# Three of nine experts of each pair of sequences run inside the next pair's layers, with the pair loop written out

## The chip, the cores and the metric

The kernel runs on one core of one Trainium2 chip. A core has five engines with an instruction stream each: TensorE (PE: matmuls and transposes; its weight loads are listed apart as PEld), VectorE (DVE), ScalarE (ACT), GpSimd (POOL) and SyncE (SP, which here only issues DMAs). They wait for one another through semaphores. The metric is the device time of one execution, in microseconds (us); lower is better.

## The reference, cut to what matters

Eight sequences of 256 tokens with 128 features pass through four layers. The change touches only the last stretch, in which two sequences (a pair, 512 tokens) are worked on together; what comes ahead is a linear-attention layer over single sequences.

```python
x = x + _L0_attn_ref(_layernorm(x), ...)      # before the pairs
x = x + _L0_ffn_ref(_layernorm(x), ...)       # 8 experts of 176 hidden + a shared one, top 2
x = x + _L1_attn_ref(_layernorm(x), ...)      # 16 heads of 8, causal, then a 128-512-128 MLP
x = x + _L1_ffn_ref(_layernorm(x), ...)       # the layer of the change:

def _L1_ffn_ref(x, shared_up, shared_down, routed_up, routed_down, router_w):
    H, F, E_SHARED, E_ROUTED, K = (128, 512, 1, 8, 2)
    def _expert(x, w_up, w_down):
        h = jax.nn.gelu(jnp.einsum('bsh,hf->bsf', x, w_up), approximate=False)
        return jnp.einsum('bsf,fh->bsh', h, w_down)
    ...                                        # gates: softmax, the two largest kept
    for e in range(E_ROUTED):
        routed_out = routed_out + gates[..., e:e + 1] * _expert(x, routed_up[e], routed_down[e])
    return shared_out + routed_out + x
```

The kernel computes all nine experts (one shared, eight routed) for all tokens, and weights each result by its gate, which is zero for an expert that was not chosen.

## The kernel before

The first half of the program (up to about 815 us) handles the eight sequences one after the other. Then come four pairs, `pair_layers(it, more)` on each engine. Pairs 0 to 2 are three rounds of a hardware loop (`Fori`), pair 3 stands behind the loop as code of its own. Order within an engine is the order of the code; there is no scheduler. One pair is, in TensorE's order:

- Start: `route(hT0, ...)` (8 columns of router scores, L1314), then 14 steps of the first feed-forward layer's up projections (L1330; each step two matmuls of 512 columns), its down projections (L1348, L1349, and L1358 to L1360) in four token chunks. VectorE adds the weighted results into `x2` chunk by chunk (L1894, L1900) and counts `merged`, once a chunk. Chunks 0 and 1 use banks 4, 5, 0, 1 of `ps` for expert results, chunks 2 and 3 banks 2 to 5; banks 6 and 7 hold the shared part.
- **Gap 1**: VectorE ends the last chunks and does two layer norms (`norm`, L1559 to L1572, with the inverse root on GpSimd, L508). `turn_tokens(1, h_tok, 4)` transposes the result (L1308), ScalarE copies it to `hT` (L830), and the attention begins with `a_wqkv` (L1365), the rotation on VectorE (L1923 to L1927) and the transposes L1374.
- Attention: scores (L1394, L1400) with maxima on VectorE (L1935), turned scores (L1428, L1432), exponentials on ScalarE (L881), values (L1452), output projection `a_wo` (L1489).
- **Gap 2**: VectorE takes the projection and does norm 5; `turn_tokens(2, h_tok, 5)`; then the MLP's up matmuls (L1494), four Gelus (L895), its down matmuls (L1499).
- **Gap 3**: VectorE adds that (L1956) and does norm 6; `turn_tokens(3, h_tok, 6)`, `route(hT, m_rt)` (L1314), and the experts.
- Experts 0 to 8: `up(e)` is four matmuls of 512 columns (L1513, in the trace 8 records, since each fp32 matmul is recorded twice), ScalarE's four Gelus (L903), `down(e)` 16 matmuls of 128 columns (L1522, 32 records), and VectorE adds bank 4 or 5, times the gate, into `x2` (L1977). `up(e + 1)` stands ahead of `down(e)`. After `down(4)` stands `turn_first(it + 1)` (L1300), the next pair's first transpose.

ScalarE holds one function table at a time; `load_table` (L832) switches it early. The names that the change and the prediction use are `h_tok` (normalised tokens), `hT` (their transpose, the input of every up matmul), `hid1` (two buffers for Gelu results), `x2` (the residual sum), `rw` (gates), `mgelu`, `mup_psum`, `mdown_psum`, `mdown_used` (counts of Gelus, up matmuls, down groups and additions).

Of the kernel before, what the change touches and what calls it, by code (L numbers as in the profile page):

```python
# [61 lines left out]
N_UP = HT1 * (E + 2)  # L62
N_DOWN = E + 2
# [15 lines left out]
DVE_STEPS2 = 161  # L79
POOL_STEPS2 = 1  # L80
# [40 lines left out]
def program(nc, t, out):  # L121
# [10 lines left out]
    with ExitStack() as ctx:  # L132
# [49 lines left out]
        def carve(phase, shape, at=None):  # L182
# [78 lines left out]
        rw = sb("rw", [P, G, E + 1])  # L261
        rwT = sb("rwT", [P, G * P])
# [22 lines left out]
        hT = carve(2, [G * P])  # L285
        v_aug = carve(2, [G, AH, AV])
# [29 lines left out]
            "mup_psum mgelu mdown_psum mlp_added mdown_used x_final x_stored "  # L316
# [51 lines left out]
        def _(sp):  # L368
# [38 lines left out]
            with sp.Fori(0, PAIRS - 1) as it:  # L407

                sp.wait_ge(s["merged"], G * it + G)
                sp.dma_start(pair_in[:, :, :], pair(out, it + 1)).then_inc(s["pair_loaded"], 16)  # L410
                sp.wait_ge(s["x_final"], it + 2)
                sp.dma_start(pair(out, it), x2[:, :, :]).then_inc(s["x_stored"], 16)
            sp.wait_ge(s["x_final"], PAIRS + 1)
            sp.dma_start(pair(out, PAIRS - 1), x2[:, :, :]).then_inc(s["x_stored"], 16)
            sp.wait_ge(s["x_stored"], 16 * PAIRS + 1)
# [3 lines left out]
        def _(pool):  # L419
# [17 lines left out]
            pool.memset(pool_pad[:, 1:2], 0.0).then_inc(s["x_stored"], 1)  # L437
            pool.memset(pool_pad[:, 2:3], 0.0).then_inc(s["x_final"], 1)
# [71 lines left out]

            def pair_layers(it, more):
                me = Steps(pool, s["pool_step2"], it, POOL_STEPS2)
# [12 lines left out]
                if more:  # L525
                    inverse_root(it + 1, 0)
                    assert me.n == POOL_STEPS2, ("POOL_STEPS2", me.n)

# [6 lines left out]
            with pool.Fori(0, PAIRS - 1) as it:  # L535
                pair_layers(it, True)
            pair_layers(PAIRS - 1, False)


        @block.scalar  # L540
        def _(act):
# [274 lines left out]

            def turned_first(i):

                act.wait_ge(s["hT_psum"], i * N_HT + 1)
                act.activation(hT0, ps[:, 7, :], ACT.Copy).then_inc(s["hT_ready"], 1)  # L820

            def pair_layers(it, more):
                def transpose_out(k, gb=None):
# [3 lines left out]
                    if gb is None:  # L827
                        act.activation(hT, src, ACT.Copy).then_inc(s["hT_ready"], 1)
# [4 lines left out]
                def load_table(function):  # L833

                    act.wait_ge(s["act_step"], it * 2 + (1 if function == ACT.Exp else 2))
                    act.activation(act_pad[:, :], act_pad[:, :], function).then_inc(s["act_step"], 1)

# [16 lines left out]

                load_table(ACT.Exp)
# [35 lines left out]
                load_table(ACT.Gelu)  # L891
                transpose_out(2, gb=1)
                for i in range(HT1):
                    act.wait_ge(s["mup_psum"], it * N_UP + i + 1)
                    act.activation(hid1[0][:, i, :], ps[:, i, :], ACT.Gelu, bias=a_b1[:, i:i + 1])\  # L895
                        .then_inc(s["mgelu"], 1)
# [3 lines left out]
                for e in range(E + 1):  # L900
                    for i in range(HT1):
                        act.wait_ge(s["mup_psum"], it * N_UP + HT1 * (e + 1) + i + 1)
                        act.activation(hid1[e % 2][:, i, :], ps[:, i, :], ACT.Gelu).then_inc(s["mgelu"], 1)  # L903
# [5 lines left out]
            with act.Fori(0, PAIRS - 1) as it:  # L909
                pair_layers(it, True)  # L910
            pair_layers(PAIRS - 1, False)


        @block.tensor
        def _(pe):
# [387 lines left out]
            def pair_layers(it, more):  # L1303
# [18 lines left out]
                for k, i in enumerate(UP_ORDER):  # L1322
# [3 lines left out]
                    if k == 2:  # L1326

                        pe.wait_ge(s["x_final"], it + 1)
# [32 lines left out]

                turn_tokens(1, h_tok, 4)
# [5 lines left out]
                def turn_qk(c):  # L1368
                    pe.wait_ge(s["rot_ready"], it * G + c + 1)
                    if c >= 2:  # L1370
                        pe.wait_ge(s["qT_ready"], (it * G + c - 1) * 2)
                    for q in range(2):
# [118 lines left out]
                mm.then_inc(s["wo_psum"], 1)  # L1491
                turn_tokens(2, h_tok, 5)
                for i in range(HT1):
                    pe.matmul(ps[:, i, :], a_w1[:, i * P:(i + 1) * P], hT, start=True, stop=True)\  # L1494
                        .then_inc(s["mup_psum"], 1)
                pe.wait_ge(s["mgelu"], it * N_UP + HT1)
# [4 lines left out]
                mm.then_inc(s["mdown_psum"], 1)  # L1501

                turn_tokens(3, h_tok, 6)
# [4 lines left out]
                def up(e):  # L1508
                    for i in range(HT1):
                        if e >= 1:  # L1510

                            pe.wait_ge(s["mgelu"], it * N_UP + HT1 * e + i + 1)
                        pe.matmul(ps[:, i, :], m_up[:, e, i * P:(i + 1) * P], hT, start=True, stop=True)\  # L1513
                            .then_inc(s["mup_psum"], 1)

                def down(e):
                    pe.wait_ge(s["mgelu"], it * N_UP + HT1 * (e + 2))
                    if e >= 2:
                        pe.wait_ge(s["mdown_used"], it * E + e - 1)
                    for c in range(G):  # L1520
                        for i in range(HT1):
                            mm = pe.matmul(ps[:, 4 + e % 2, c * P:(c + 1) * P], hid1[e % 2][:, i, c * P:(c + 1) * P],  # L1522
# [550 lines left out]
```

## Time and profile before

| | |
|---|---|
| Median of 3 timed runs | 1685.59 us (1682.43 to 1690.14) |
| Profiled execution: its own time | 1669.67 us |
| Its span in the trace | 1667.9 us |
| TensorE matmul busy | 1368.3 us (82%), 11040 instructions |
| TensorE weight load busy | 984.9 us (59%) |
| VectorE busy | 911.9 us (55%) |
| ScalarE busy | 723.2 us (43%) |
| GpSimd busy | 195.3 us (12%) |
| Granted TensorE clock, mean of the span | 0.843 |

Busy shares are of the whole span. A granted clock of 1.00 is 2.4 GHz and one of 0.50 is 1.2 GHz; a number between them is a stretch that holds both. In the trace, "idle before <-releaser" is the time for which an engine stood still ahead of an instruction and what ended it; "issue" there means that nothing the profile shows ended it. Ends of matmuls are modelled; the start of the next one is the firmer number.

### The profile page before, as it was taken

Reading aid. Unit: us, or ns where it says so; the run is one execution under the profiler, and the core shown is the slowest. Engines: PE = TensorE matmul, PEld = TensorE weight load, DVE = VectorE, ACT = ScalarE, POOL = GpSimd, SP = SyncE. Lnnn points to the kernel's source line nnn. Section 1 sums busy time; section 2 is a strip of 40 time slices with the busy share of each in tenths; the row PEclk is TensorE's granted clock in tenths of the full one; section 3 lists DMA queues with packets and bytes.
Section 4 is the critical chain, followed back from the end, with each engine's and each line's share of the span. In section 5 each row is a group of like instructions: output and inputs, shape, how many; then the busy total and the mean of one; then the engine's idle time right before and its main releaser. Section 6 shows DMA issues by size and latency. Waiting matters only on the chain.

```text
span 1667.9 us, 27801 instructions
## 1 busy us (share of the span) xinstructions
PE 1368.3 (82%) x11040; PEld 984.9 (59%) x11048; DVE 911.9 (55%) x2365; ACT 723.2 (43%) x1347; POOL 195.3 (12%) x188
## 2 busy tenths in 40 slices
PE   2768897988879888878588789877899768997689
PEld 2456666676757667568455466653676435764356
DVE  4687979787887969681354222552224621255221
ACT  1646473746565564724232333423324233342332
POOL 5011212112121212110100000000000000000000
PEclk9768898887978787876796899968999689996899
DMA  3000000000000000003000000000000000000000
GB/s 113 4 1 4 2 11 1 1 10 2 10 2 10 2 7 2 29 1 138 12 7 1 1 1 8 1 7 1 1 8 1 7 1 1 7 1 1 1 0 7
DMA packets 15076, 17.80 MB, mean 11 GB/s; under 512 B 2567, under 2 KB 13216, under 8 KB 14560
## 3 DMA queue, kind: packets, MB, share of 16 engines
q1 hardware_dynamic: 12768, 14.09, 2.6%
q8 instruction: 91, 1.49, 0.4%
q0 software_dynamic: 576, 1.76, 0.3%
q10 hardware_dynamic: 1600, 0.12, 0.1%
q14 instruction: 41, 0.34, 0.1%
HBM read 13.87 MB, written 2.10 MB: 10 GB/s over the span
## 4 chain that ended last, share of the span: by engine, by line
PE 36%; issue 32%; DVE 23%; ACT 6%; POOL 2%; DMA 1%; SPq 0%; POOLq 0%; DVEq 0%; ACTq 0%
PE ps L1012 4%; DVE arena L1677 4%; DVE arena L1680 4%; PE ps L1513 4%; PE ps L1522 4%; PE ps L994 4%; DVE arena L1595 2%; PE ps L1494 1%; PE ps L1330 1%; PE ps L979 1%; POOL rstd L508 1%; PE ps L1138 1%; ACT arena L611 1%; PE ps L991 1%; PE ps L1125 1%
## 5 line engine op out<-in xcount | busy, mean ns | idle before, releaser
L1595 DVE SCALAR_TENSOR_TENSOR arena<-ps,conv_w,arena 128x255 f32<-128x255 f32 (+2 forms) x384 | 163.6, 475 | 19.5 <-ACT arena L602 15.0
L1522 PEld LDWEIGHTS ps<-arena 128*128 128x128 f32 x1152 | 133.7, 192 | 15.3 <-issue 14.6
L903 ACT ACTIVATE arena<-ps 128x512 f32<-128x512 f32 x144 | 86.0, 597 | 127.9 <-PE ps L1513 127.9
L1513 PE MATMUL ps<-arena 128*128 128x512 f32 x288 | 135.3, 617 | 0.0
L1522 PE MATMUL ps<-arena 128*128 128x128 f32 x1152 | 133.8, 275 | 0.0
L1977 DVE SCALAR_TENSOR_TENSOR arena<-ps,rw,arena 128x128 f32<-128x128 f32 x128 | 36.0, 343 | 139.0 <-PE ps L1522 139.0
L508 POOL TENSOR_TENSOR rstd<-var_eps,half_power 128x2 f32<-128x2 f32 (+1 forms) x28 | 23.3, 832 | 748.2 <-DVE var_eps L1566 748.2
L1012 PE MATMUL ps<-arena 64*128 64x256 f32 x256 | 84.0, 468 | 16.4 <-ACT arena L611 16.4
L1012 PEld LDWEIGHTS ps<-arena 64*128 64x128 f32 x256 | 53.4, 225 | 62.3 <-DVE arena L1665 27.2
L1663 DVE TENSOR_TENSOR arena<-ps,arena 128x512 f32<-128x512 f32 x64 | 44.1, 689 | 84.2 <-PE ps L1012 73.9
L468 POOL TENSOR_TENSOR arena<-con,log_decay 128x512 f32<-128x512 f32 x64 | 68.3, 1078 | 178.4 <-PE ps L994 78.5
L1513 PEld LDWEIGHTS ps<-arena 128*128 128x128 f32 x288 | 55.0, 200 | 57.1 <-issue 57.1
L979 PE MATMUL ps<-arena 128*128 128x256 f32 x256 | 80.7, 450 | 8.8 <-DVE arena L1595 8.0
L1680 DVE TENSOR_TENSOR arena<-arena 128x30 f32<-128x30 f32 (+14 forms) x240 | 83.1, 346 | 8.2
L1677 DVE TENSOR_TENSOR arena<-arena 128x30 f32<-128x30 f32 (+14 forms) x240 | 83.0, 346 | 7.0
L994 PE MATMUL ps<-arena,con 128*128 128x512 f32 x128 | 83.8, 743 | 0.0
L581 ACT ACTIVATE arena<-ps,log_beta 128x128 f32<-128x128 f32 x256 | 70.9, 378 | 29.0 <-PE ps L994 28.7
L1308 PE MATMUL ps<-con,h_tok 128*128 128x128 f32 x48 | 13.4, 435 | 82.0 <-DVE h_tok L1572 82.0
L979 PEld LDWEIGHTS ps<-arena 128*128 128x128 f32 x256 | 53.6, 226 | 31.1 <-DVE arena L1595 17.9
L482 POOL TENSOR_TENSOR o_rstd<-ssq,half_power 128x16 f32<-128x16 f32 x16 | 47.0, 2936 | 212.6 <-DVE ssq L1715 212.6
L602 ACT ACTIVATE arena<-ps,conv_w 128x256 f32<-128x256 f32 x128 | 51.7, 485 | 44.9 <-PE ps L979 44.6
L1935 DVE TENSOR_REDUCE arena<-ps 128x8 f32<-128x2048 f32 (+1 forms) x24 | 54.3, 2289 | 30.6 <-PE ps L1400 30.6
(247 smaller groups left out, 2988.5 us busy)
## 6 DMA issues: line engine op xcount, KB each, us to landing
arena<-in_routed_up SPq DMA_DIRECT2D x1, 2048.0 KB, 9.9
arena<-in_routed_down SPq DMA_DIRECT2D x1, 2048.0 KB, 14.5
x_ln<-in_x SPq DMA_DIRECT2D x8, 128.0 KB, 2.3
arena<-in_w_mix SPq DMA_DIRECT2D x1, 1024.0 KB, 9.7
x_in<-in_x SPq DMA_DIRECT2D x8, 128.0 KB, 2.5
out_x<-x_res SPq DMA_DIRECT2D x8, 128.0 KB, 1.9
arena<-out_x SPq DMA_DIRECT2D x4, 256.0 KB, 2.7
out_x<-arena SPq DMA_DIRECT2D x4, 256.0 KB, 3.3
```

The lines of the kernel that those rows point to most:

```text
L468: pool.tensor_tensor(gm[k % NB].rearrange("p (h n) -> p h n", h=BATCH), over_heads(upto, BATCH), over_last(log_decay[n % 2][:, c, BATCH * ...
L581: ins = act.activation(dm[n % 2][:, BATCH * k + h, :], ps[:, k % 2, h * P:(h + 1) * P], ACT.Exp, bias=log_beta[n % 2][:, c, v:v + 1])
L903: act.activation(hid1[e % 2][:, i, :], ps[:, i, :], ACT.Gelu).then_inc(s["mgelu"], 1)
L979: mm = pe.matmul(ps[:, PAIR_BANK[p], j * SEQ:(j + 1) * SEQ], w_mix[:, m * P:(m + 1) * P], hT3[:, f % 3, :], start=True, stop=True)
L994: pe.matmul(ps[:, k % 2, :], beyond, gm[k % NB], start=False, stop=True, skip_group_check=True)\
L1012: mm = pe.matmul(ps[:, KK_BANK[k % 2], 2 * P * g:2 * P * (g + 1)].rearrange("p (q n) -> p q n", q=2), mix_qk[n % 2][r:r + DH, QK_TILES + m ...
L1513: pe.matmul(ps[:, i, :], m_up[:, e, i * P:(i + 1) * P], hT, start=True, stop=True)\
L1522: mm = pe.matmul(ps[:, 4 + e % 2, c * P:(c + 1) * P], hid1[e % 2][:, i, c * P:(c + 1) * P], m_down[:, e, i, :], start=(i == 0), stop=(i == ...
L1595: ins = dve.scalar_tensor_tensor(conv_tile(f, m)[:, sh:SEQ], ps[:, PAIR_BANK[p], j * SEQ:(j + 1) * SEQ - sh], conv_w[:, m, TAPS - 1 - sh:T ...
L1677: me.did(dve.tensor_tensor(tmp, inv[:, j + 1:BLOCK, j:j + 1].to_broadcast([P, rows, j]), inv[:, j:j + 1, 0:j].to_broadcast([P, rows, j]), ...
L1680: me.did(dve.tensor_tensor(inv[:, j + 1:BLOCK, 0:j], inv[:, j + 1:BLOCK, 0:j], tmp, ALU.subtract))
L1935: dve.tensor_reduce(heads, sc, X_AXIS, ALU.max, negate=True).then_inc(s["max_ready"], 1)
```

## The change

For a pair that has a successor, experts 6, 7 and 8 (`LATE`) are no longer computed at the pair's end. Each is computed in one of the three gaps of the next pair, up, Gelu, down and addition. In gap 1 the up matmuls share banks 0 and 1 (`LATE_BANKS[0]`), so the third and fourth wait for a Gelu; in gaps 2 and 3 each has its own bank. Down goes to bank 6, 6 and 5. The last pair computes all nine at its end. Since the next pair overwrites `x2`, `hT` and `rw`, the expert layer gets buffers of its own: `x_m`, `hT_m` and `gates`. The hardware loops are gone: the pairs are written out on every engine. ScalarE gets one more switch of tables in pairs 1 to 3 (Gelu for gap 1, and back to Exp), and SP stores pair `it - 1` after gap 3 of pair `it`.

```diff
+UP_BANKS = (0, 1, 2, 3)
+LATE_BANKS = ((0, 1, 0, 1), (1, 2, 3, 5))
+LATE_DOWN = (6, 6, 5)
+LATE = (EXPERTS - 3, EXPERTS - 2, EXPERTS - 1)
...
# SP
+                if it > 0:
+                    sp.wait_ge(s["mdown_used"], EXPERTS * it)
+                    sp.dma_start(pair(out, it - 1), x_m[:, :, :]).then_inc(s["x_stored"], 16)
...
# ScalarE
+                def hidden(p, e, banks, half):
+                    q = EXPERTS * p + e
+                    for i in range(HT1):
+                        act.wait_ge(s["mup_psum"], HT1 * q + i + 1)
+                        act.activation(hid1[half][:, i, :], ps[:, banks[i], :], ACT.Gelu).then_inc(s["mgelu"], 1)
...
+                if it > 0:
+                    load_table(ACT.Gelu)
+                    hidden(it - 1, LATE[0], LATE_BANKS[0], 0)
                 load_table(ACT.Exp)
                 transpose_out(1, gb=0)
...
                 load_table(ACT.Gelu)
+                if it > 0:
+                    hidden(it - 1, LATE[1], LATE_BANKS[1], 1)
                 transpose_out(2, gb=1)
...
# TensorE
-                    if k == 2:
-                        pe.wait_ge(s["x_final"], it + 1)
+                    if k == 2 and it > 0:
+                        pe.wait_ge(s["mdown_used"], EXPERTS * (it - 1) + LATE[0])
...
+                def up(p, e, banks):
+                    q = EXPERTS * p + e
+                    for i in range(HT1):
+                        if banks[i] in banks[:i]:
+                            pe.wait_ge(s["mgelu"], HT1 * q + i - 1)
+                        elif 1 <= e < LATE[0] or (e >= 1 and not more and p == it):
+                            pe.wait_ge(s["mgelu"], HT1 * (q - 1) + i + 1)
+                        pe.matmul(ps[:, banks[i], :], m_up[:, e, i * P:(i + 1) * P], hT_m, start=True, stop=True)\
+                            .then_inc(s["mup_psum"], 1)
+                def down(p, e, bank, half):
+                    q = EXPERTS * p + e
+                    pe.wait_ge(s["mgelu"], HT1 * (q + 1))
+                    after(pe, "mdown_used", q - 1)
...
+                if it > 0:
+                    pe.wait_ge(s["merged"], it * G + 2)
+                    up(it - 1, LATE[0], LATE_BANKS[0])
+                    pe.wait_ge(s["merged"], it * G + G)
+                    down(it - 1, LATE[0], LATE_DOWN[0], 0)
                 turn_tokens(1, h_tok, 4)
...
+                if it > 0:
+                    up(it - 1, LATE[1], LATE_BANKS[1])
+                    down(it - 1, LATE[1], LATE_DOWN[1], 1)
                 turn_tokens(2, h_tok, 5)
...
+                if it > 0:
+                    up(it - 1, LATE[2], UP_BANKS)
+                    down(it - 1, LATE[2], LATE_DOWN[2], 1)
 
                 turn_tokens(3, h_tok, 6)
-                route(hT, m_rt[:, :])
+                route(hT_m, m_rt[:, :])
...
-            with pe.Fori(0, PAIRS - 1) as it:
-                pair_layers(it, True)
-            pair_layers(PAIRS - 1, False)
+            for it in range(PAIRS):
+                pair_layers(it, it + 1 < PAIRS)
...
# VectorE
+                def accumulate(p, e, bank):
+                    q = EXPERTS * p + e
+                    dve.wait_ge(s["mdown_psum"], q + 1)
+                    after(dve, "mdown_used", q)
...
+                    for c in range(G):
+                        ins = dve.scalar_tensor_tensor(x_m[:, c, :], ps[:, bank, c * P:(c + 1) * P],
+                                                       gates[:, c, e - 1:e], x_m[:, c, :], ALU.mult, ALU.add)
...
+                if it > 0:
+                    accumulate(it - 1, LATE[0], LATE_DOWN[0])
                 dve.memset(qk_tok[:, :, 1, :, AD:AD + 1], 1.0)
...
                 norm(5, xp, h_tok)
+                if it > 0:
+                    accumulate(it - 1, LATE[1], LATE_DOWN[1])
...
                 norm(6, x2, h_tok)
+                if it > 0:
+                    accumulate(it - 1, LATE[2], LATE_DOWN[2])
                 route(1, False)
```

What moves on TensorE at gaps 2 and 3. First the order before, from the attention's output projection (L1489) to the first experts of a looped pair (L1513 up, L1522 down; REGISTER_ALU and ISA rows compute what a wait in the loop waits for):

```order
L1489 MATMUL ps<-arena 128x128 x4
L1306 REGISTER_ALU
L1308 MATMUL ps<-con,h_tok 128x128 x4
L1494 MATMUL ps<-arena 128x512 x4
L1496 ISA
L1499 MATMUL ps<-arena 128x128 x16
L1306 REGISTER_ALU
L1308 MATMUL ps<-con,h_tok 128x128 x4
L1314 MATMUL ps<-m_rt,arena 128x8 x4
L1513 MATMUL ps<-arena 128x512 x4
```

And now, in pair 2, the same place in the changed kernel (L1539 is the output projection, L1390 an expert's up, L1399 its down, L1327 a transpose of tokens, L1547 and L1552 the MLP, L1333 the router):

```order
L1539 MATMUL ps<-arena 128x128 x4
L1390 MATMUL ps<-arena 128x512 x4
L1399 MATMUL ps<-arena 128x128 x16
L1327 MATMUL ps<-con,h_tok 128x128 x4
L1547 MATMUL ps<-arena 128x512 x4
L1552 MATMUL ps<-arena 128x128 x16
L1390 MATMUL ps<-arena 128x512 x4
L1399 MATMUL ps<-arena 128x128 x16
L1327 MATMUL ps<-con,h_tok 128x128 x4
L1333 MATMUL ps<-m_rt,arena 128x8 x4
L1390 MATMUL ps<-arena 128x512 x8
```

An expert (up and down) now stands ahead of each of the two transposes, so the transpose, and what follows it, is queued behind the expert. In gap 1 the same pair of rows stands between the last down projection of the first feed-forward layer (L1379) and the transpose:

```order
L1377 MATMUL ps<-w,arena 128x128
L1378 MATMUL ps<-w2r,arena 128x128
L1379 MATMUL ps<-b,rwT 128x128
L1390 MATMUL ps<-arena 128x512 x4
L1399 MATMUL ps<-arena 128x128 x16
L1327 MATMUL ps<-con,h_tok 128x128 x4
```

On VectorE the additions stand behind the norms. This is the order of the changed kernel in gap 1, where L1610 is a norm's last step, L1880 the late expert's additions and L1973 the first step of the attention's rotation:

```order
L1602 BN_AGGR mv<-stats 128x2 x2
L1604 TENSOR_SCALAR var_eps<-mv 128x2
L1610 TENSOR_SCALAR h_tok<-arena,mv,rstd 128x128 x2
L1880 SCALAR_TENSOR_TENSOR arena<-ps,gates,arena 128x128 x4
L1973 MEMSET arena 128x4x16
```

Before, the memset followed the norm directly; now the rotation is queued behind a wait for the late expert's down matmuls.

## Rows read from the trace of the kernel before

**Rows 1.** The page: busy shares, and the granted clock in 40 slices.

```profile
PE 1368.3 (82%) x11040; PEld 984.9 (59%) x11048; DVE 911.9 (55%) x2365; ACT 723.2 (43%) x1347; POOL 195.3 (12%) x188
...
PEclk9768898887978787876796899968999689996899
```

**Rows 2.** Timeline, pair 0, expert stream: start, us, engine, line, op, [idle before].

```profile
1015.25 3.60 PE L1513 MATMUL ps<-arena 128*128 128x512 f32 x8
...
1016.30 0.60 ACT L903 ACTIVATE arena<-ps 128x512 f32<-128x512 f32 x1 [3.83 <-PE ps L1513]
...
1018.68 3.73 PE L1522 MATMUL ps<-arena 128*128 128x128 f32 x32
...
1018.88 0.60 ACT L903 ACTIVATE arena<-ps 128x512 f32<-128x512 f32 x1 [0.26 <-PE ps L1513]
...
1022.25 3.60 PE L1513 MATMUL ps<-arena 128*128 128x512 f32 x8
```

**Rows 3.** Stretches of pair 1: length, busy PE PEld DVE ACT POOL, PEclk, DMA, GB/s.

```profile
1080.30:1083.50 3.20, 0.00 (x0) 0.00 (x0) 3.20 (x14) 0.00 (x0) 0.00 (x0) 1.00 0.00 0
...
1089.65:1097.10 7.45, 6.58 (x13) 3.65 (x14) 3.25 (x12) 1.61 (x4) 0.00 (x0) 0.50 0.00 0
...
1107.40:1121.10 13.70, 12.73 (x91) 8.80 (x93) 9.51 (x5) 1.65 (x3) 0.00 (x0) 0.50 0.00 1
...
1175.80:1182.50 6.70, 6.01 (x16) 3.93 (x17) 2.37 (x17) 3.99 (x5) 1.27 (x1) 0.50 0.00 1
```

**Rows 4.** Timeline of gap 1 in pair 1, VectorE first, then TensorE.

```profile
1080.53 4.22 DVE L1900 SCALAR_TENSOR_TENSOR arena<-ps,rw,arena 128x128 f32<-128x128 f32 x16
...
1093.63 0.42 DVE L1923 TENSOR_TENSOR arena<-ps,con 128x256 f32<-128x256 f32 x1 [3.92 <-ACT arena L859]
...
1079.90 0.39 PE L1360 MATMUL ps<-b,rwT 128*128 128x128 f32 x2
1089.65 1.12 PE L1308 MATMUL ps<-con,h_tok 128*128 128x128 f32 x4 [9.36 <-DVE h_tok L1572]
1091.64 5.49 PE L1365 MATMUL ps<-arena 128*128 128x384 f32 x8 [0.87 <-ACT arena L830]
```

**Rows 5.** Timeline of gap 2 in pair 1, TensorE and ScalarE's table.

```profile
1150.79 1.28 ACT L836 ACT_TABLE_LOAD   x1
...
1150.82 1.16 PE L1489 MATMUL ps<-arena 128*128 128x128 f32 x8 [0.69 <-ACT arena L890]
...
1158.54 1.11 PE L1308 MATMUL ps<-con,h_tok 128*128 128x128 f32 x4 [6.56 <-DVE h_tok L1572]
...
1160.53 6.10 PE L1494 MATMUL ps<-arena 128*128 128x512 f32 x8 [0.87 <-ACT arena L830]
...
1167.40 3.84 PE L1499 MATMUL ps<-arena 128*128 128x128 f32 x32 [0.78 <-ACT arena L895]
```

**Rows 6.** Timeline of gap 3 in pair 1, TensorE.

```profile
1175.81 1.12 PE L1308 MATMUL ps<-con,h_tok 128*128 128x128 f32 x4 [4.57 <-DVE h_tok L1572]
...
1179.34 8.66 PE L1513 MATMUL ps<-arena 128*128 128x512 f32 x16
...
1187.83 3.73 PE L1522 MATMUL ps<-arena 128*128 128x128 f32 x32
```

**Rows 7.** Timeline, pair starts after loop branch and after loop exit; gap-1 transposes.

```profile
1035.06 1.32 PE L1314 MATMUL ps<-gate_w,arena 128*128 128x8 f32 x8 [2.06 <-issue]
...
1301.34 1.12 PE L1308 MATMUL ps<-con,h_tok 128*128 128x128 f32 x4 [9.37 <-DVE h_tok L1572]
...
1456.08 0.96 PE L1314 MATMUL ps<-gate_w,arena 128*128 128x8 f32 x8
...
1508.90 1.12 PE L1308 MATMUL ps<-con,h_tok 128*128 128x128 f32 x4 [9.37 <-DVE h_tok L1572]
```

**Rows 8.** Timeline, pair 0: transpose L1300 inside the expert stream, and its copy.

```profile
1007.80 0.60 PE L1300 MATMUL ps<-con,h_tok 128*128 128x128 f32 x4
...
1008.44 0.60 ACT L820 ACTIVATE arena<-ps 128x512 f32<-128x512 f32 x1 [3.41 <-PE ps L1300]
```

More of the change, by code:

```diff
@@ L534, in _ @@
             pool.memset(v_aug[:, :, :, AD:AD + 1], 1.0)
-            with pool.Fori(0, PAIRS - 1) as it:
-                pair_layers(it, True)
-            pair_layers(PAIRS - 1, False)
+            for it in range(PAIRS):
+                pair_layers(it, it + 1 < PAIRS)
         @block.scalar
@@ L908, in _ @@
             turned_first(0)
-            with act.Fori(0, PAIRS - 1) as it:
-                pair_layers(it, True)
-            pair_layers(PAIRS - 1, False)
+            for it in range(PAIRS):
+                pair_layers(it, it + 1 < PAIRS)
         @block.tensor
@@ L1360, in pair_layers @@
                     pe.matmul(o, rwT[:, cs], b2[:, :], start=False, stop=True).then_inc(s["down_psum"], 1)
+                def up(p, e, banks):
[12 more added lines that the diff above has]
+                    for c in range(G):
+                        for i in range(HT1):
+                            mm = pe.matmul(ps[:, bank, c * P:(c + 1) * P], hid1[half][:, i, c * P:(c + 1) * P],
+                                           m_down[:, e, i, :], start=(i == 0), stop=(i == HT1 - 1))
+                    mm.then_inc(s["mdown_psum"], 1)
+                if it > 0:
[3 more added lines that the diff above has]
+                    down(it - 1, LATE[0], LATE_DOWN[0], 0)
                 turn_tokens(1, h_tok, 4)
@@ L1500, in pair_layers @@
                                        start=(i == 0), stop=(i == HT1 - 1))
-                mm.then_inc(s["mdown_psum"], 1)
-                turn_tokens(3, h_tok, 6)
+                mm.then_inc(s["fdown_psum"], 1)
                 pe.wait_ge(s["w_d_in"], 16 * 3)
                 pe.wait_ge(s["m_down_in"], 16 * 2)
-                route(hT, m_rt[:, :])
[L1508 to L1522, printed above, removed]
-                                           m_down[:, e, i, :], start=(i == 0), stop=(i == HT1 - 1))
-                    mm.then_inc(s["mdown_psum"], 1)
-                up(0)
-                for e in range(E + 1):
-                    if e < E:
-                        up(e + 1)
-                    down(e)
+                if it > 0:
+                    up(it - 1, LATE[2], UP_BANKS)
+                    down(it - 1, LATE[2], LATE_DOWN[2], 1)
+                turn_tokens(3, h_tok, 6)
+                route(hT_m, m_rt[:, :])
+                up(it, 0, UP_BANKS)
+                here = LATE[0] if more else EXPERTS
+                for e in range(here):
+                    if e + 1 < here:
+                        up(it, e + 1, UP_BANKS)
+                    down(it, e, 4 + e % 2, e % 2)
                     if more and e == AHEAD:
```

103 lines of the change are left out of this document (49 added, 54 removed).

## Prediction

> **What bounds the kernel now.** I read the page first: TensorE's matmuls are busy 82% of the span, no other engine over 55%, and the row of the granted clock moves between 6 and 9 tenths from the middle on [rows 1]. So there are two losses to look for in the pairs, idle TensorE and slow TensorE. The timeline of the experts shows TensorE without a gap and at the full clock: an expert's up starts at 1015.25 and the next one's at 1022.25, so an expert costs 7.00 us (3.43 up, 3.57 down), and ScalarE and VectorE follow with time to spare [rows 2]. An expert at a pair's end is therefore pure TensorE time, and taking it away takes 7.00 us away. The gaps are the opposite: in gap 1 TensorE waits 9.36 us for a norm [rows 4], in gap 2 6.56 us [rows 5], in gap 3 4.57 us [rows 6]; 20.5 us a pair. The stretches show the second loss: the clock is still 1.00 in the first 3.2 us of gap 1, but what follows it runs at 0.50 (1089.65 to 1097.10), and so it is behind gap 3 (1175.80 to 1182.50) and, in a row like these two, behind gap 2. The middle of the attention is a third kind: 0.50 with TensorE busy 12.73 of 13.70 us [rows 3]. Ahead of the falls at the gaps TensorE had stood still; ahead of the attention's it had not.
>
> **The terms.** All is worked out on pair 1, and then taken three times: pairs 1, 2 and 3 have filled gaps, pairs 0, 1 and 2 lose three experts each.
>
> *Removed from the ends.* 9 x 7.00 = **-63.0 us**. That the stream stays TensorE's is safe: six experts in place have the same waits as nine, and the fourth Gelu ends well before down needs it [rows 2].
>
> *The loop.* At the branch TensorE stands still 2.06 us for nothing that the profile shows, and VectorE, ScalarE and TensorE begin the next pair together [rows 7]. After pair 2 the loop ends and the next code simply follows. The same transposes of gap 1 start at 1089.65 in pair 1 [rows 4], at 1301.34 in pair 2 and at 1508.90 in pair 3 [rows 7]: 211.69 us with a branch between, 207.56 without. So a branch costs 4.13 us (stall, a slower clock after it, router matmuls of 1.32 us instead of 0.96). Two branches are taken: **-8.3 us**. Pair 3 in the trace is straight code and starts without a stall, so I take nothing for unrolled code. The next pair's third step now waits for the sixth addition; it starts about 4.2 us after the last down (0.8 router, two steps of 1.71), the addition is through after 1.3 us: nothing.
>
> *A late expert by itself.* Up(e) has no other down behind which its Gelus hide. From the stream: first Gelu 1.05 us after the first matmul, the fourth ends at 1018.88 + 0.60, which is 4.23 us after 1015.25 [rows 2]. Down starts then, at 4.3 us, and the next TensorE instruction 3.57 us later. So a late expert holds TensorE's queue 7.9 us at the full clock. Each Gelu is on ScalarE, which is idle in all three gaps.
>
> *Gap 1.* TensorE's last down projection starts at 1079.90, so up starts at 1080.1. Its banks 0 and 1 belong to the chunks that VectorE has long merged (it begins the second half at 1080.53). The third matmul waits for the first Gelu (1081.75), which costs a few tenths: fourth matmul from about 1082.8, last Gelu at 1084.5. Down waits for the last merge, 1080.53 + 4.22 = 1084.75 [rows 4], and holds the queue to 1088.5. The transposes start at 1089.65 because the norm ends there; they are **not delayed**, with 1.1 us to spare. The additions (four of about 0.28 us) stand on VectorE between the norm and the rotation, where it waits 3.92 us anyway [rows 4]. ScalarE's two table loads of 1.28 us [rows 5] fall before the up matmuls and after the last Gelu, at 1086: hidden. If the clock then stays full, the transposes take 0.64 us until their copy instead of about 1.15 (the same four transposes at the full clock: start 1007.80, copy 1008.44 [rows 8]), and the first qkv chunk, a quarter of 5.49 us, halves. The rotation on VectorE, which paces what follows, starts 0.5 + 0.65 = **1.15 us earlier**.
>
> *Gap 2.* The projection starts at 1150.82; its eight records leave TensorE free at 1151.8. The Gelu table is in at 1152.1, before the first Gelu's turn at 1152.9. The expert holds the queue until 1159.7, and the transposes started at 1158.54 [rows 5]: **+1.15**. Behind them, warm: -0.5 for the transposes; MLP up to MLP down took 6.87 us at the half clock (1160.53 to 1167.40), and by the rows of a warm up with its Gelus 4.3 (one Gelu with bias is about 0.1 longer): -2.5. Sum **-1.85**.
>
> *Gap 3.* The MLP's down starts at 1167.40, leaves TensorE free at 1170.97, and the expert holds it until 1178.9, where the transposes started at 1175.81 [rows 6]: **+3.05**. From the transposes to the first up it took 3.53 us [rows 6]; warm that is 0.64 to the copy and 0.60 of copy [rows 8], 0.05, and 0.85 of the router's 0.96 us [rows 7], 2.15: -1.4. Two ups took 1187.83 - 1179.34 = 8.49 us [rows 6] and warm take 6.86: -1.6. Sum **+0.1**. The additions fall between norm 6 and the router's logits, at about 1180, and end before the logits come.
>
> **Sum:** -63.0 - 8.3 + 3 x (-1.15 - 1.85 + 0.1) = **-80 us**. Against the profiled execution (1669.67 us, of it 1667.9 span) that is 1589.7, and a span of about 1588. The median of the timed runs, 1685.59, lies 15.9 us above the profiled one; the change touches nothing that I can see in that difference, so I subtract from the median: **1605.6 us**.
>
> **Two rules weighed.** ScalarE's table load took 1.28 us here [rows 5]. The Trainium skill (*ScalarE: Activation LUTs*, What ACT_TABLE_LOAD costs) adds a drain of about 1.38 us to every switch, about 2.66 us in all. By that rule the table of gap 2 would be in at 1153.45 and the first Gelu about 0.5 us late, an estimate from that page; three pairs would lose 1.6 us, and the sum would be -78. The sum goes by the row. On the clock, the skill (*TensorE: Matmul & The Clock Gate*, Part 1) says that a clock gate follows how busy the engine has been lately; by that rule a gap that is only partly filled can lose the clock again, which is the second rival and its 1626.9 us.
>
> **Rivals.**
> 1. *As summed*: experts and what follows run mostly at 2.4 GHz. For it: the clock falls at all three gaps behind a full stop of 4.6 us or more, and in the new gaps no stop is longer than about 1.3 us. Chance 0.66.
> 2. *The experts fit, but the clock falls all the same behind them.* The transposes and their copy leave TensorE nearly idle for two microseconds, and in the attention the clock is down although TensorE is hardly ever idle [rows 3]. Then nothing is given back: gap 1 0, gap 2 +1.15, gap 3 +3.05, sum -63.0 - 8.3 + 12.6 = -58.7, **1626.9 us**. Chance 0.23.
> 3. *The branches' price stays* (the stall is a matter of each engine's queue and comes with new code too, or the attention loses elsewhere what the start gains): -80 + 8.3 = -71.7, **1613.9 us**. Pair 3 speaks against it. Chance 0.08.
> 4. *No gain, the other side: the late experts themselves run at 1.2 GHz.* Up and down double: matmuls of 1.71 us, fourth Gelu at 7.6 us, down 7.1, so TensorE's queue is held 14.8 us. Gap 1: 1080.1 + 14.8 = 1094.9, +5.25; gap 2 +8.1; gap 3 +9.95; three pairs 69.9. With -63.0 and, if straight code stalls as the branch did, no gain of the loop: **+7 us, 1692 us**; with the loop's gain 1684. It decides from about 13 us of hold per expert on. Against it: the clock was 1.00 at the start of each gap (1080.30 to 1083.50) [rows 3]. Chance 0.03.
> That the change does not do what it says has no room: the order of instructions shows the experts in the gaps.
>
> **How the numbers follow.** Likeliest: 1605.6. Its own bounds: the attention's clock is the open one, since its falls may shift with all that comes earlier. At the full clock VectorE's 9.51 us of work would set the pace of the 13.70 us stretch [rows 3], so it could give up to 4.2 us a pair, -93 at the low end; half of what is given back behind the gaps lost, -70 at the high end. The timed runs differ from each other by 8 us and from the profile by 16. For the range I take 1590 to 1632: the low end is the -93 with some of the spread of a timed run, the high end holds rivals 2 and 3 with the same spread. A change of 0.5% (8.4 us), about what a measurement of this kernel can tell from no change, is passed in all cases but the fourth: faster 0.97, same 0.02, slower 0.01.
>
> **What would show each step.** The span from one gap-1 transpose to the next should be about 211.7 - 4.1 - 21.0 - 2.9 = 183.7 us from pair 1 to 2, and the same from pair 2 to 3, where no branch stood. The start of a pair: no idle ahead of the router matmuls. Gap 1: the transposes' releaser still VectorE's norm; gaps 2 and 3: TensorE's own order (no wait for `h_tok`). PEclk near 1.00 in the three stretches behind the gaps. It would be wrong if down in gap 1 ends after the norm, if PEclk shows 0.50 behind the gaps, or if VectorE's additions hold back the rotation or the router.

## The result, and the profile after

The changed kernel takes 1602.8 us (median of four timed runs, 1596.3 to 1604.2) against 1684.0 us (1676.7 to 1690.1): ratio 0.953, 95% interval 0.950 to 0.956. The forecast was 1605.6 us, ratio 0.953. The profiled execution took 1602.93 us with a span of 1601.1, 66.8 us less than that of before, not 80. Where the missing 13 us are is told at the end of this section and under the prediction, and it is the most instructive part.

The page after. Busy share of TensorE up from 82% to 85%, and the row of the clock in 40 slices, which answers to [rows 1]:

```profile
PE 1360.9 (85%) x11048; PEld 979.9 (61%) x11048; DVE 911.8 (57%) x2365; ACT 727.3 (45%) x1353; POOL 194.6 (12%) x186
...
PEclk9768779797887979896659679995999979997999
```

Gap 1 of pair 1 in the timeline (columns as in [rows 4]; L1390 is a late expert's up, L1399 its down, L1327 the transposes, L1959 the merge, L1880 the late additions, L1984 the rotation):

```profile
1060.94 3.69 PE L1390 MATMUL ps<-arena 128*128 128x512 f32 x8
1061.35 4.22 DVE L1959 SCALAR_TENSOR_TENSOR arena<-ps,rw,arena 128x128 f32<-128x128 f32 x16
...
1064.67 0.60 ACT L851 ACTIVATE arena<-ps 128x512 f32<-128x512 f32 x1 [0.26 <-PE ps L1390]
...
1065.62 3.84 PE L1399 MATMUL ps<-arena 128*128 128x128 f32 x32 [0.98 <-DVE arena L1959]
...
1070.33 1.12 DVE L1880 SCALAR_TENSOR_TENSOR arena<-ps,gates,arena 128x128 f32<-128x128 f32 x4
1070.47 0.66 PE L1327 MATMUL ps<-con,h_tok 128*128 128x128 f32 x4 [1.01 <-DVE h_tok L1610]
...
1072.00 4.54 PE L1412 MATMUL ps<-arena 128*128 128x384 f32 x8 [0.87 <-ACT arena L837]
...
1073.86 0.42 DVE L1984 TENSOR_TENSOR arena<-ps,con 128x256 f32<-128x256 f32 x1 [2.29 <-ACT arena L877]
```

The whole expert lies inside the wait. Its down waits 0.98 us for the last merge, and behind it the transposes still wait 1.01 us for the norm: the expert costs nothing. VectorE still waits 2.29 us ahead of the rotation, so the additions cost nothing either. The rotation starts 3.39 us after the transposes instead of 3.98 [rows 4]; in pairs 2 and 3 (not shown) it is 2.78 us.

Gaps 2 and 3, TensorE alone, pair 3 (L1539 output projection, L1547 and L1552 the MLP, L1333 the router); answers to [rows 5] and [rows 6]:

```profile
1505.29 1.16 PE L1539 MATMUL ps<-arena 128*128 128x128 f32 x8 [0.69 <-ACT arena L908]
1506.29 3.60 PE L1390 MATMUL ps<-arena 128*128 128x512 f32 x8
1510.57 3.84 PE L1399 MATMUL ps<-arena 128*128 128x128 f32 x32 [0.69 <-ACT arena L851]
1514.25 0.60 PE L1327 MATMUL ps<-con,h_tok 128*128 128x128 f32 x4
1515.71 3.70 PE L1547 MATMUL ps<-arena 128*128 128x512 f32 x8 [0.87 <-ACT arena L837]
...
1520.19 3.84 PE L1552 MATMUL ps<-arena 128*128 128x128 f32 x32 [0.78 <-ACT arena L915]
1523.87 3.60 PE L1390 MATMUL ps<-arena 128*128 128x512 f32 x8
1528.15 3.84 PE L1399 MATMUL ps<-arena 128*128 128x128 f32 x32 [0.69 <-ACT arena L851]
1531.83 0.60 PE L1327 MATMUL ps<-con,h_tok 128*128 128x128 f32 x4
1533.12 1.06 PE L1333 MATMUL ps<-m_rt,arena 128*128 128x8 f32 x8 [0.69 <-ACT arena L835]
1534.03 7.11 PE L1390 MATMUL ps<-arena 128*128 128x512 f32 x16
1540.98 3.73 PE L1399 MATMUL ps<-arena 128*128 128x128 f32 x32
```

The transposes (1514.25, 1531.83) have no wait any more: TensorE's own queue is what holds them. From the projection to the transposes it is 8.96 us instead of 7.72; from the transposes to the MLP's down 5.94 instead of 8.86; from there to the next transposes 11.64 instead of 8.41; to the first expert's up 2.20 instead of 3.53, and from that up to its down 6.95 instead of 8.49.

The granted clock (third number from the right) behind gaps 2, 3 and 1 of pair 1, where [rows 3] has 0.50 behind gaps 1 and 3:

```profile
1145.30:1151.25 5.95, 4.31 (x14) 1.80 (x12) 1.13 (x4) 3.53 (x5) 0.00 (x0) 1.00 0.00 0
1162.89:1172.04 9.15, 8.46 (x30) 4.40 (x29) 3.97 (x23) 7.33 (x11) 0.00 (x0) 1.00 0.10 29
1070.47:1076.37 5.90, 5.03 (x12) 2.81 (x13) 3.43 (x13) 1.61 (x4) 0.00 (x0) 0.71 0.00 0
```

The start of pair 3, after down(5) (L1399), with nothing between it and the router's matmuls:

```profile
1388.71 3.74 PE L1399 MATMUL ps<-arena 128*128 128x128 f32 x32
1392.29 0.96 PE L1333 MATMUL ps<-gate_w,arena 128*128 128x8 f32 x8
```

Four stretches of the changed kernel: length, busy time by engine with counts (PE, PEld, DVE, ACT, POOL), granted clock, DMA share, GB/s. Each runs from the gap-1 transposes to the output projection, and so holds the attention of pair 0, 1, 2 and 3:

```profile
882.41:945.01 62.60, 55.49 (x512) 33.96 (x512) 23.10 (x35) 21.43 (x43) 0.00 (x0) 0.74 0.00 1
1070.47:1136.35 65.88, 59.73 (x513) 35.64 (x513) 24.13 (x39) 21.44 (x43) 0.00 (x0) 0.66 0.00 1
1260.47:1320.99 60.52, 52.25 (x513) 32.01 (x513) 24.03 (x39) 21.66 (x43) 0.00 (x0) 0.80 0.00 1
1445.11:1505.29 60.18, 52.15 (x512) 31.65 (x513) 24.03 (x39) 21.44 (x43) 0.00 (x0) 0.80 0.01 1
```

The same code takes 60.2 to 65.9 us, in step with its granted clock (0.80 to 0.66). Before, pairs 0 to 2 took 61.1 to 61.2 us each at 0.77, and I had taken that sameness for a property of the code. The nine traces in this document whose attention is the same code keep this order: from 57.7 us at 0.85 over 58.1 to 58.8 at 0.83 and 63.4 to 63.6 at 0.71 to 66.4 us at 0.65.

The terms in the two traces, in us: experts and branches -71.1 (down(0) to the next router: 58.88 on average in pairs 0 and 1, 56.63 in pair 2, now 35.61 in all; router to the gap-1 transposes 54.60 twice, now 52.82); gaps 2 and 3, 3 x (1.24 - 2.91 + 3.23 - 1.33 - 1.54) = -3.9; the attention of pairs 1 to 3 +2.4 (186.6 against 184.2), that of pair 0 +1.4; and the gap-1 transposes of pair 0, behind code that the change leaves alone but for two small memsets, come at 882.4 instead of 878.1, +4.4. Sum -66.8. Of the 13.2 us to the forecast's -80, the attention of pairs 1 to 3 makes 5.8 (+2.4 where -3.45 was forecast), pair 0 and what lies ahead of it 5.8, and gaps 2 and 3 1.4 (-3.9 where -5.25 was forecast).

### The profile page after: what moved, and what is told of

Same layout as the page of the kernel before. It is cut to its first block, busy times and chain, and to the rows that moved or that the text cites. A ratio compares the mean times of both kernels' runs of the same rounds, so it can differ in the third digit from the quotient of the medians.

```text
span 1601.1 us, 26853 instructions
## 1 busy us (share of the span) xinstructions
PE 1360.9 (85%) x11048; PEld 979.9 (61%) x11048; DVE 911.8 (57%) x2365; ACT 727.3 (45%) x1353; POOL 194.6 (12%) x186
## 4 chain that ended last, share of the span: by engine, by line
PE 61%; DVE 24%; ACT 9%; issue 3%; POOL 1%; DMA 1%; SPq 0%; DVEq 0%; ACTq 0%
PE ps L1399 7%; PE ps L1390 7%; PE ps L1349 6%; PE ps L1031 5%; DVE arena L1715 4%; PE ps L1013 4%; DVE arena L1718 4%; PE ps L1482 2%; DVE arena L1959 2%; PE ps L1450 2%; ACT arena L899 2%; PE ps L1157 2%; PE ps L1089 2%; PE ps L1502 1%; PE ps L998 1%
## 5 line engine op out<-in xcount | busy, mean ns | idle before, releaser
L851 ACT ACTIVATE arena<-ps 128x512 f32<-128x512 f32 x144 | 85.3, 597 | 162.1 <-PE ps L1390 162.0
L1399 PEld LDWEIGHTS ps<-arena 128*128 128x128 f32 x1152 | 133.2, 192 | 25.5 <-issue 11.0
L1399 PE MATMUL ps<-arena 128*128 128x128 f32 x1152 | 135.2, 276 | 7.1 <-ACT arena L851 4.1
L1390 PE MATMUL ps<-arena 128*128 128x512 f32 x288 | 131.0, 600 | 0.0
L1880 DVE SCALAR_TENSOR_TENSOR arena<-ps,gates,arena 128x128 f32<-128x128 f32 x128 | 36.0, 344 | 131.4 <-PE ps L1399 131.4
L1390 PEld LDWEIGHTS ps<-arena 128*128 128x128 f32 x288 | 52.5, 193 | 55.2 <-issue 50.8
L998 PE MATMUL ps<-arena 128*128 128x256 f32 x256 | 76.6, 431 | 7.8 <-DVE arena L1633 7.1
L899 ACT ACTIVATE arena<-ps 128x512 f32<-128x512 f32 x96 | 49.6, 602 | 52.9 <-PE ps L1482 52.9
L2000 DVE COPY arena<-ps 128x512 f32<-128x512 f32 x16 | 10.3, 687 | 109.5 <-PE ps L1502 109.5
L1157 PE MATMUL ps<-arena 128*128 128x64 f32 x512 | 69.9, 301 | 0.0
```

What stands on the lines that cost most here:

```text
L851: act.activation(hid1[half][:, i, :], ps[:, banks[i], :], ACT.Gelu).then_inc(s["mgelu"], 1)
L899: act.activation(probsT[u % 2][:, j, :], ps[:, 4 + j, :], ACT.Exp).then_inc(s["probs_ready"], 1)
L998: mm = pe.matmul(ps[:, PAIR_BANK[p], j * SEQ:(j + 1) * SEQ], w_mix[:, m * P:(m + 1) * P], hT3[:, f % 3, :], start=True, stop=True)
L1157: mm = pe.matmul(ps[:, (7, 5)[g], h * DH:(h + 1) * DH], dm[i % 2][:, VH * c + v, :], eps[:, v, :], start=True, stop=True)
L1390: pe.matmul(ps[:, banks[i], :], m_up[:, e, i * P:(i + 1) * P], hT_m, start=True, stop=True)\
L1399: mm = pe.matmul(ps[:, bank, c * P:(c + 1) * P], hid1[half][:, i, c * P:(c + 1) * P], m_down[:, e, i, :], start=(i == 0), stop=(i == HT1 - 1))
```

## The experiments

Each stands beside runs of the kernel before on the same chip; the last three ran on another chip than the rest, so they are compared with the rest by their ratios. "Stretch" below is always the one from the gap-1 transposes to the output projection.

**Only the loop written out.** From the kernel before, on every engine:

```diff
-            with pe.Fori(0, PAIRS - 1) as it:
+            for it in range(PAIRS - 1):
                 pair_layers(it, True)
             pair_layers(PAIRS - 1, False)
```

> The kernel before with only the loop over pairs written out on every engine. Theory (each taken branch costs 4.1 us of the start of a pair): two branches go, so about -8.3 us against before, ratio 0.995; in the trace no idle time for 'issue' ahead of the router matmuls of pairs 1 and 2, and from one gap-1 transpose to the next 207.6 us each time. Rival (the stall belongs to new code and not to the branch): the same 2.06 us stand at each pair's start, ratio 1.000.

Measured: 1668.7 us, ratio 0.993 (0.990 to 0.996). The start of pair 1 in its trace:

```profile
1039.75 0.72 PE L1522 MATMUL ps<-arena 128*128 128x128 f32 x5
1040.31 0.96 PE L1314 MATMUL ps<-gate_w,arena 128*128 128x8 f32 x8
1041.12 1.11 PE L1330 MATMUL ps<-arena 128*128 128x512 f32 x2
```

The 2.06 us of idle time are gone, and from down(0) of a pair to the gap-1 transposes of the next it takes 109.45 us in all of them, against 113.5 with a branch: 4.0 us each, 4.1 forecast. The timed runs gained 12 us (7 to 17) where 8.3 were forecast. New code does not stall. But the second half of my expectation failed: from one gap-1 transpose to the next it is 211.0, 205.0 and 209.6 us, not 207.6 each time, since the stretches are 63.5, 58.1, 63.4 and 61.8 us.

**Nothing moved, only the clock.** On top of that kernel, in pairs 1 to 3 (gaps 1, 2 and 3 in this order). The results are read by nobody:

```diff
+                def keep_warm(banks, n):
+                    for i in range(n):
+                        pe.matmul(ps[:, banks[i % len(banks)], :], m_up[:, 0, 0:P], hT0, start=True, stop=True)
+                if it > 0:
+                    pe.wait_ge(s["merged"], it * G + 2)
+                    keep_warm((0, 1), 10)
                 turn_tokens(1, h_tok, 4)
...
+                    keep_warm((1, 2, 3, 5), 7)
                 turn_tokens(2, h_tok, 5)
...
+                    keep_warm((0, 1, 2, 3), 5)
                 turn_tokens(3, h_tok, 6)
```

> As e1, and in the gaps of pairs 1 to 3 TensorE also does 10, 7 and 5 matmuls of 512 columns whose results nobody reads (nothing is moved away from the pairs' ends). They fit into the waits, so what this kernel gains over e1 is what the clock alone gives back. Theory: what stands behind a filled gap runs at 2.4 GHz, -2.9 us behind gap 2, -2.9 us behind gap 3, -1.15 us behind gap 1, three pairs, about -21 us against e1 and -29 us against before, ratio 0.983. Rival (the clock falls behind the gap all the same, in the transposes): as e1, ratio 0.995.

Measured: 1652.1 us, ratio 0.985 (0.982 to 0.988), so -14 us against the first experiment (1678.6 x (0.9929 - 0.9847)); with the two intervals put together, between 7 and 21. More work on TensorE, less time. The rival is out: from the gap-2 transposes to the MLP's down it takes 6.0 us in every filled pair, instead of 8.0 to 8.8 in the first experiment, all at 2.4 GHz. Pair 1:

```profile
1155.52:1161.53 6.01, 4.36 (x13) 1.86 (x13) 0.00 (x0) 3.52 (x5) 0.00 (x0) 1.00 0.00 0
```

The trace shows where about 5 of the expected 21 us stayed: behind gap 3 the clock did fall once more (in pair 1 from 1172.2 to 1175.6), at the end of the router matmuls, and from the first up to the first down it took 8.6 us in each of the three pairs instead of the 6.95 of the changed kernel.

**One late expert, gap 1 only.** From the changed kernel, with the calls for `LATE[1]` and `LATE[2]` taken out on all engines:

```diff
-LATE = (EXPERTS - 3, EXPERTS - 2, EXPERTS - 1)
+LATE = (EXPERTS - 1,)
```

> The changed kernel with one late expert instead of three, in gap 1; gaps 2 and 3 empty. Theory: gap 1 takes an expert for nothing, so 3 x 7.0 = 21 us and the branches 8.3, and up to 3 x 1.15 of clock: -29 to -33 us against before, ratio 0.980 to 0.983. Rival (filling gap 1 makes the attention behind it slower, as in pair 1 of the changed kernel, where it took 65.9 instead of 61.2 us): -29 + 5 to 14 us, ratio 0.986 to 0.991, and in the trace the stretch from the gap-1 transposes to the output projection is over 62.5 us in pairs 1 to 3.

Measured: 1644.8 us, ratio 0.979 (0.976 to 0.982), -35 us. The rival, over 62.5 us behind the filled gap, is refuted in this trace: it is 58.7 us, less than the 61.1 to 61.9 of before.

```profile
1082.63:1141.38 58.75, 50.29 (x510) 30.64 (x512) 24.08 (x39) 21.56 (x43) 0.00 (x0) 0.83 0.02 6
1280.64:1339.36 58.72, 50.30 (x510) 30.64 (x513) 24.10 (x39) 21.55 (x43) 0.00 (x0) 0.83 0.02 6
1478.61:1537.34 58.73, 50.30 (x511) 30.65 (x513) 24.09 (x39) 21.56 (x43) 0.00 (x0) 0.83 0.02 6
```

**Two late experts, gaps 2 and 3 only.** From the changed kernel, with all calls for gap 1 and the wait for its addition taken out:

```diff
-LATE = (EXPERTS - 3, EXPERTS - 2, EXPERTS - 1)
+LATE = (EXPERTS - 2, EXPERTS - 2, EXPERTS - 1)
```

> The changed kernel with two late experts instead of three, in gaps 2 and 3; gap 1 empty. Theory: 6 x 7.0 = 42 us, the branches 8.3 us, and in sum -1.3 us a pair at gaps 2 and 3 (hold of the queue +1.2 and +3.2, clock -2.9 and -2.9): -54 us against before, ratio 0.968, with the attention at 61.2 us in all pairs as before, since gap 1 is as it was. Rival (the attention's time wanders with whatever comes earlier, gap 1 filled or not): the attention differs from 61.2 us in this trace too.

Measured: 1629.1 us, ratio 0.969 (0.965 to 0.974), -52 us. Gaps 2 and 3 show the very same times as in the changed kernel (8.96, 5.95, 11.64, 2.20, 6.95 us). The attention, with gap 1 as it was before the change, wanders all the same, and pair 0, the same work as before, is the slowest of all kernels. Pairs 0 and 1:

```profile
880.80:947.24 66.44, 59.91 (x511) 36.14 (x513) 23.09 (x35) 21.43 (x43) 0.00 (x0) 0.65 0.00 1
1079.55:1141.97 62.42, 54.93 (x511) 33.70 (x513) 23.09 (x35) 21.54 (x43) 0.00 (x0) 0.74 0.00 1
```

So the wandering does not come from filling gap 1. The parts add up: -35 and -52 us, less the -12 us of the loop that both hold, is -75 us. The whole measured -81 in the result and -75 in the repeat that follows, so they add up inside the intervals.

**The changed kernel again.** Not edited.

> The changed kernel once more, unaltered, beside the kernels below on the same chip. All theories: ratio to before 0.953 within 0.004. If the attention's time wanders with the position of the clock's steps and not with the code, its stretches (gap-1 transposes to output projection) in this trace differ from those of the first trace of the same kernel, 62.6, 65.9, 60.5 and 60.2 us.

Measured: 1604.5 us, ratio 0.955 (0.952 to 0.959). The stretches were 63.55, 60.65, 60.53 and 60.12 us instead of 62.60, 65.88, 60.52 and 60.18. One program, two executions, 5 us apart in one place. The first stretch began at 890.6 us instead of 882.4, and in the thirteen traces of all kernels, whose first half is all but the same, it began between 876.5 and 890.6.

**Pair 0 kept warm too.** The changed kernel, with the same `keep_warm` (on `w1` in place of `m_up`) in pair 0, which has no late experts:

```diff
+                if it == 0:
+                    keep_warm((1, 2, 3, 5), 7)
                 turn_tokens(2, h_tok, 5)
```

and likewise 10 and 5 matmuls in gaps 1 and 3.

> The changed kernel, and in pair 0, whose gaps have no late expert, TensorE does 10, 7 and 5 matmuls of 512 columns in gaps 1, 2 and 3 whose results nobody reads. Theory (what a filled gap gives back is the clock): -2.9 us behind gap 2, -2.9 us behind gap 3, up to -1.15 us behind gap 1, so -6 to -7 us against the changed kernel, ratio to before 0.949; in the trace pair 0 shows 5.95 us instead of 8.8 from the gap-2 transposes to the MLP's down matmuls. Rival: no change, since the attention takes back what comes early.

Measured: 1591.4 us (1589.0 to 1594.8), ratio 0.948 (0.945 to 0.952); no run of the unaltered kernel on this chip was under 1598.8. Behind gap 2 of pair 0 it took 6.00 us, against 8.45 in the trace of the unaltered kernel just above. The 13 us between the medians are more than the 7 forecast; in the traces pair 0's own gaps give 5.0 (2.45 + 1.24 + 1.27), and its attention 3.8 (59.7 against 63.55). How much of the latter is this edit and how much the wandering, two traces cannot tell.

**More full-row work in the attention.** The changed kernel, with each mask matmul done twice, in `scores` and `turned_scores`:

```diff
+                        for _ in range(2):
                             pe.matmul(out_j[:, :, c * P:(c + 1) * P], ident_bf[:, :], causal_bf[:, 0:n, :],
                                       start=True, stop=False, skip_group_check=True)
```

> The changed kernel with each causal-mask matmul of the attention (bf16, all 128 rows) done twice in all pairs; the second starts the same sum afresh, so values are as before. It adds 16384 columns a pair, 6.8 us at 2.4 GHz and 13.7 at 1.2, partly in waits. Theory (the clock falls in the attention because its matmuls use 8 or 9 rows of the array, not because TensorE is idle): with more full-row work the clock falls less, the cold time in a pair's attention goes from 20 to 41 us to under 14, and the stretch of 60 to 66 us gets to 55 to 59, ratio to before 0.940 to 0.950. Rival (rows have nothing to do with it): the clock is as it was, the stretch gets longer by 5 to 13 us, ratio 0.965 to 0.985.

and with `range(3)`:

> As the kernel with each mask matmul twice, but three times (32768 columns a pair more than the changed kernel). Theory: the clock stays at 2.4 GHz through scores and turned scores, but the added 13.7 us at that clock lie partly on the path: stretch of 58 to 63 us. Rival (clock as it was): stretch of 72 us and more, ratio to before over 0.98.

Measured: 1598.6 us, ratio 0.952 (0.948 to 0.955), and 1602.5 us, ratio 0.955 (0.950 to 0.960), neither to be told from the changed kernel (0.955). The stretches of pairs 1 and 3 with masks twice, and of pair 1 with masks three times:

```profile
1072.47:1133.07 60.60, 53.05 (x560) 31.75 (x560) 24.05 (x39) 21.21 (x43) 0.00 (x0) 0.92 0.01 1
...
1441.82:1501.53 59.71, 51.81 (x561) 30.57 (x561) 24.05 (x39) 21.42 (x43) 0.00 (x0) 0.94 0.01 2
```

```profile
1072.44:1133.85 61.41, 54.85 (x609) 34.71 (x609) 24.23 (x39) 21.43 (x43) 0.00 (x0) 1.00 0.01 1
```

Half right: the clock follows (0.92 to 0.94 in all four pairs, then 0.93 to 1.00, instead of 0.80), the time does not. At a clock of 1.00 throughout, pair 1's stretch is still 61.4 us, and the other three took 62.1 to 63.5: the added work takes at least what the clock gives. My hope for 55 to 59 us fell. Only pair 0 with masks twice, 58.2 us, lies in it, and one stretch of a kind that wanders by itself proves nothing.

**Combinations.** Masks twice and pair 0 warm, on the changed kernel:

> The changed kernel with the matmuls nobody reads in pair 0's gaps and each causal-mask matmul done twice, both edits together. Theory (both act on the clock, at different places): the gains add, -13 and -6 us, about 1585 us, ratio to before 0.944; attention stretches of 58 to 60.6 us in all pairs. Rival (both gain by the same thing, that the attention of pair 0 or 1 no longer falls into a long cold stretch): no better than the pair-0 matmuls alone, ratio 0.948.

Measured: 1595.8 us, ratio 0.947 (0.943 to 0.951): no better than pair 0 warm alone (0.948). The rival's number came, and no gain of the masks can be told from nothing. The stretches of its trace, 60.3, 61.3, 63.7 and 60.5 us, miss the expected 58 to 60.6 in two pairs.

The last idea comes from what gaps 2 and 3 show above: the queue is held too long there. The transposes go inside the late expert's down matmuls:

```diff
                     for c in range(G):
+                        if c == before_chunk:
+                            turn_issue(h_tok, ln)
                         for i in range(HT1):
                             mm = pe.matmul(ps[:, bank, c * P:(c + 1) * P], hid1[half][:, i, c * P:(c + 1) * P],
...
-                    down(it - 1, LATE[1], LATE_DOWN[1], 1)
+                    down(it - 1, LATE[1], LATE_DOWN[1], 1, 3, 5)
...
-                    down(it - 1, LATE[2], LATE_DOWN[2], 1)
+                    down(it - 1, LATE[2], LATE_DOWN[2], 1, 1, 6)
```

> The changed kernel with the matmuls in pair 0's gaps, and in gaps 2 and 3 the transposes of the normalised tokens go into the late expert's down matmuls (ahead of the last of its four chunks in gap 2, ahead of the second in gap 3), so that ScalarE's copy runs beside the rest. Theory (in gaps 2 and 3 TensorE's queue is held longer than the norm takes, by 1.2 and 3.2 us, and each microsecond of that is on the path): the MLP's up starts 0.95 us earlier, the experts' first up 0.9 us earlier, three pairs, -5.5 us against the pair-0 matmuls alone, ratio 0.945. Rival (the attention or ScalarE takes it back): 0.948.

Measured: 1584.6 us, ratio 0.943 (0.939 to 0.946). In gap 3 of pair 3 (L1393 up, L1404 down, L1326 transposes, L1336 router):

```profile
1499.75 3.60 PE L1393 MATMUL ps<-arena 128*128 128x512 f32 x8
1504.04 1.16 PE L1404 MATMUL ps<-arena 128*128 128x128 f32 x8 [0.69 <-ACT arena L851]
1505.03 0.60 PE L1326 MATMUL ps<-con,h_tok 128*128 128x128 f32 x4
1505.47 2.84 PE L1404 MATMUL ps<-arena 128*128 128x128 f32 x24
1508.15 0.96 PE L1336 MATMUL ps<-m_rt,arena 128*128 128x8 f32 x8
1508.96 7.11 PE L1393 MATMUL ps<-arena 128*128 128x512 f32 x16
```

The wait for ScalarE's copy (0.69 us, ahead of the router in the changed kernel) is gone, since it runs beside the other three chunks. From the MLP's down to the experts' first up it takes 12.88 us instead of 13.84, and from the output projection to the transposes 8.06 instead of 8.96: 1.86 us a pair, 1.85 forecast. The difference of the ratios to pair 0 warm alone, 0.9482 to 0.9427, is 9 us; 5.6 of them are this, the rest is within what intervals of 0.35% allow.

> All three edits together: matmuls in pair 0's gaps, mask matmuls twice, transposes inside the late experts' down. If they add: -13 - 6 - 5.5 against the changed kernel, about 1580 us, ratio to before 0.941. If masks and pair-0 matmuls gain by the same thing: 0.945.

Measured: 1581.7 us, ratio 0.941 (0.938 to 0.945), not to be told from the one without masks. Of the two I would keep the simpler, at 0.943: about 1% better than the changed kernel.

## Why the prediction was right

Its likeliest case came true: 1602.8 us for 1605.6. The mechanism is borne out step by step, but that the two numbers lie within 3 us is luck in part. The sum of -80 was worked out in one trace and then taken from a median 15.9 us above it, as if that offset would stay. It did not: the profiled execution of the changed kernel lies at its median (1602.9 against 1602.8), the one of the kernel before 14 us below its own (1669.7 against 1684.0). The terms in the traces came out 13 us short of the forecast, and the offset that vanished made up for it. By its own steps:

- *Removed from the ends*, -63.0: exact. From the first down to the next pair's router it took 21.02 us less where no branch stood, three times 7.0.
- *The loop*, -8.3: right, 8.1 in the traces, and -12 us (-7 to -17) in the timed runs of the kernel with nothing else changed.
- *Gap 1*, transposes not delayed with 1.1 us to spare: right, 1.01. Of the 1.15 us by which the rotation should start earlier, pair 1 got 0.6, since the clock fell to 0.50 at 1072.2 for a few microseconds; pairs 2 and 3, where it did not, got 1.2.
- *Gap 2*: hold +1.24 (forecast +1.15), behind it -2.91 (-3.0). *Gap 3*: hold +3.23 (+3.05), behind it -2.87 (-3.0). Both right to 0.2 us. The time of a single expert, 7.9 us from the four rows of the stream, was 7.96.
- *Which rule priced the table.* The first Gelu of gap 1 came 1.06 us after its matmul's start, and the table was long there; in gap 2 down started 4.28 us after up, as the 1.28 us load of [rows 5] has it. The additional drain of the Trainium skill (*ScalarE: Activation LUTs*, What ACT_TABLE_LOAD costs) would have made it about 4.8, an estimate from that page; here it cost nothing that shows: in pair 3 the load starts at 1505.26 and an activation follows it at 1506.55.
- *Rival 2*, the clock falls behind the filled gaps: refuted behind gaps 2 and 3 of the changed kernel (1.00 in all three pairs), true in small behind gap 1, and behind gap 3 of the kernel with unread matmuls, where the clock fell once in each pair.
- *Rivals 3 and 4.* The written-out loop has no stall at pairs 1 and 2, so the branches' price did go; that the attention loses something elsewhere came true in small, as the next point says. The late experts did not run at 1.2 GHz: those of gaps 2 and 3 held the queue 7.96 us each, not 14.8.
- *The attention* was mis-sized, in both directions: I gave it a gain of 1.15 us a pair in the sum, up to 4.2 more in the range, and no loss. In the traces it lost 2.4 us over pairs 1 to 3, and it wanders between 57.7 and 66.4 us in kernels whose attention is the same code. So a single trace of this kernel carries several microseconds of it, and the first half of the program another plus or minus 7. That this is also what parts the -67 us of the profiled executions from the -81 of the timed runs is likely, but with one trace of the kernel before it is not shown.
- *From one gap-1 transpose to the next*, 183.7 us forecast: 190.0 from pair 1 to 2, 5.9 of the 6.3 too many in pair 1's attention, and 184.6 from pair 2 to 3.

What places the clock's steps in the attention is not settled. That they follow what TensorE does there, and not idle time alone, is shown by the kernels with more mask work: in pair 1 the clock was 0.92 and 1.00, with TensorE idle for 7.6 and 6.6 us of about 61, against 0.80 in pair 2 of the changed kernel with 8.3 us idle. Nothing here shows how to make the stretch short on purpose: it was 58.7 us three times running with one late expert, and 62.4 to 63.4 three times with two.

## What to carry to other kernels

A wait on the engine that bounds the kernel cost twice here, by its length and by the slower clock behind it, so work that is needed anyway is best put there, and even unneeded work paid: 22 unread matmuls in each of three pairs gained 14 us. Size such a filler by how long it holds the engine's queue (7.9 us for an expert alone, against 7.0 in the stream), compare that with the wait, and let what the next stage needs overtake inside the filler. When loop rounds look alike to a tenth of a microsecond, that need not be the code's own time: move anything, and the clock's steps fall elsewhere, so judge effects of a few microseconds by segments of the trace that hold no such step, or by many timed runs.

## What the runs showed of the hardware

- A taken branch over the pair's code cost 4.0 us: 2.06 us in which TensorE stood still for nothing that the profile shows (2.12 at the second branch), and a slower clock right after it, 0.53 on average from 1035.5 to 1039.0. The same code as a straight run had neither. The Trainium skill (*Runtime: NRT & Kernel Launch*, Instruction fetch mechanics) says that a taken branch to a distant target breaks the sequential fetch of instructions and stalls; the traces agree with the stall; that fetching is its cause no trace shows.
- A granted clock of 1.00 over a whole attention stretch, got by added work, did not make it shorter than at 0.80 without that work: 61.4 us against 60.1 to 60.7. Raising the clock is not an aim by itself.
- One program's attention stretch took 65.9 us in one execution (clock 0.66) and 60.7 us in another (0.80), while three rounds of the loop of before agreed within 0.05 us in one trace.
